# The small constant of an RMS norm as a 129th column of the squares, in a kernel of attention and a gated feed-forward

## What is computed

```python
def _rmsnorm(t, w):
    var = jnp.mean(t * t, axis=-1, keepdims=True)
    return t * jax.lax.rsqrt(var + EPS) * w      # EPS = 1e-06, 128 elements in the last axis
...
q = _rope(_rmsnorm(q, q_norm_w), pos)
k = _rope(_rmsnorm(k, k_norm_w), pos)
```

## Time and profile before

| | us |
|---|---|
| median of 3 runs | 1514.4 |
| lowest and highest | 1512.0, 1514.88 |
| span of the profiled execution | 1372.6 |
| TensorE busy | 1356.7 (99%) |
| VectorE busy | 1204.1 (88%) |
| ScalarE busy | 871.6 (64%) |
| GpSimd busy | 785.0 (57%) |

### The profile page before, as it was taken

The page is one execution under the profiler, slowest core; times in us unless marked ns, Lnnn a source line. Parts: engine busy times, 40 slices in busy tenths (PEclk is TensorE's granted clock), DMA queues, the critical chain, the costliest instruction groups (busy, mean ns, idle before and its releaser), DMA issues.

```text
span 1372.6 us, 23448 instructions
## 1 busy us (share of the span) xinstructions
PE 1356.7 (99%) x8015; PEld 1182.3 (86%) x8015; DVE 1204.1 (88%) x2624; ACT 871.6 (64%) x2224; POOL 785.0 (57%) x813
## 2 busy tenths in 40 slices
PE   8899999999999999999999999999999999999998
PEld 6788888888888888888888888888888888888888
DVE  8999898989898989898989898989899987987783
ACT  7777676767676767676767676767777662222221
POOL 7876766676667666766676667666766510111111
PEclk9999999999999999999999999999999999999999
DMA  6111221111112111211111112112121321111212
GB/s 215 48 53 41 59 55 47 43 59 55 47 43 59 54 47 43 58 55 47 43 59 53 49 42 59 55 47 70 49 72 32 110 96 45 47 47 49 76 40 77
DMA packets 34034, 80.46 MB, mean 59 GB/s; under 512 B 10258, under 2 KB 11538, under 8 KB 32498
## 3 DMA queue, kind: packets, MB, share of 16 engines
q1 hardware_dynamic: 17522, 45.29, 10.5%
q0 software_dynamic: 16384, 33.59, 8.4%
HBM read 76.74 MB, written 2.10 MB: 57 GB/s over the span
## 4 chain that ended last, share of the span: by engine, by line
PE 91%; DVE 5%; ACT 2%; issue 1%; POOL 1%; DMA 0%; DVEq 0%; ACTq 0%
PE proj_ps L111 10%; PE proj_ps L113 10%; PE proj_ps L112 10%; PE turn_ps L770 10%; PE score_ps L113 5%; PE score_ps L112 5%; PE score_ps L111 5%; PE value_ps L111 5%; PE value_ps L112 5%; PE value_ps L113 5%; PE gu_ps L111 3%; PE gu_ps L113 3%; PE gu_ps L112 3%; PE out_ps L1035 2%; PE turn_ps L732 2%; PE turn_ps L739 2%
## 5 line engine op out<-in xcount | busy, mean ns | idle before, releaser
L1286 ACT ACTIVATE probs<-probs,shift,rstd 128x640 f32<-128x640 f32 x256 | 234.4, 917 | 123.3 <-DVE shift L1730 122.2
L561 POOL DMA_INDIRECT kg<-kc,idx x256 | 260.1, 1016 | 83.9 <-issue 78.0
L571 POOL DMA_INDIRECT vg<-vc,idx x256 | 260.0, 1016 | 70.7 <-issue 70.7
L1766 DVE TENSOR_TENSOR pt_lo<-turn_ps,pt_hi 128x512 fp32r<-128x512 f32 x320 | 217.4, 685 | 45.2 <-ACT pt_hi L1292 44.8
L1292 ACT ACTIVATE pt_hi<-turn_ps 128x512 fp32r<-128x512 f32 x320 | 187.5, 593 | 90.6 <-PE turn_ps L770 89.3
L1741 DVE CUSTOM_DVE_ANT_0 probs<-score_ps,mask 128x640 f32<-128x640 f32 x256 | 206.8, 822 | 11.9 <-PE score_ps L113 10.1
L579 POOL TENSOR_TENSOR v_lo<-vg,v_hi 128x512 fp32r<-128x512 f32 x64 | 89.1, 1392 | 207.7 <-ACT v_hi L1257 207.7
L770 PE MATMUL turn_ps<-cst,probs 128*128 128x128 f32 x1280 | 191.5, 272 | 0.7 <-DVE qt_lo L1718 0.7
L111 PE MATMUL proj_ps<-w_hi,xt_parts 128*128 128x512 f32 x496 | 188.9, 381 | 0.0
L770 PEld LDWEIGHTS turn_ps<-cst,probs 128*128 128x128 f32 x1280 | 157.2, 141 | 26.9 <-DVE probs L1759 1.0
L113 PE MATMUL proj_ps<-w_hi,xt_parts 128*128 128x512 f32 x496 | 168.1, 339 | 0.0
(11 more groups left out here) (255 smaller groups left out, 3283.4 us busy)
## 6 DMA issues: line engine op xcount, KB each, us to landing
w_raw<-wqkv SPq DMA_DIRECT2D x28, 384.0 KB, 3.2
wo_raw<-wo SPq DMA_DIRECT2D x32, 256.0 KB, 3.0
wa_sb<-wa SPq DMA_DIRECT2D x7, 1024.0 KB, 4.9
kg<-kc,idx POOLq DMA_INDIRECT x256, 2.6
vg<-vc,idx POOLq DMA_INDIRECT x256
wg_raw<-wg SPq DMA_DIRECT2D x2, 1376.0 KB, 6.1
wu_raw<-wu SPq DMA_DIRECT2D x1, 2752.0 KB, 9.6
wd_raw<-wd SPq DMA_DIRECT2D x1, 2560.0 KB, 12.8
```

Source lines behind the costliest of these rows:

```text
L561: pool.indirect_dma_start(kg[:, b % 2, c, :], None, kc, bass.IndirectOffsetOnAxis(ap=idx[:, s // B % 2, b * NC + c:b * NC + c + 1], axis=0))\
L571: pool.indirect_dma_start(vg[:, b % 2, c, :], None, vc, bass.IndirectOffsetOnAxis(ap=idx[:, s // B % 2, b * NC + c:b * NC + c + 1], axis=0))\
L1286: act.activation(row, row, ACT.Exp, bias=shift[:, h:h + 1], scale=rstd[:, b % 2, h:h + 1], accum_out=sums[:, h:h + 1])\
L1766: dve.tensor_tensor(pt_lo[:, at, :], turn_ps[1 - j % 2][:, :], pt_hi[:, at, :].bitcast(F32), ALU.subtract).then_inc(p_lo_done[j], 1)
```

## The change

Each of the five rows of `qk` gets a 129th element, filled once by GpSimd in the setup with the square root of 128 * EPS. ScalarE squares and sums 129 elements, so the sum in `ss` already holds 128 * EPS. GpSimd's addition, the tensor `ss_eps` and the semaphore `eps_added` go, and the power reads `ss`. The squares of step s now wait for `rstd_done` of the step before in place of `eps_added`, and those of step 0 also for the setup's fills, whose count goes from 4 to 5. The copy of the queries writes four rows of 128 with a gap of one element between them; `squared`, the unused output of the squares, has rows of 129 too. Tensors that lie behind `qk` and `squared` in memory move by 32 or 64 bytes. `eps` stays, since it feeds the dummy activations that load ScalarE's tables.

```diff
--- before.py
+++ after.py
@@ -75,7 +75,7 @@
-SETUP_POOL = 4
+SETUP_POOL = 5
@@ -162,7 +162,6 @@
         squares_done = semaphore("squares_done")
-        eps_added = semaphore("eps_added")
         rstd_done = semaphore("rstd_done")
@@ -230,14 +229,15 @@
             rot_q = sb("rot_q", [P, 2, REP, D])
-            qk = sb("qk", [P, REP + 1, D])
+            qk_eps = sb("qk_eps", [P, REP + 1, D + 1])
+            qk, root_eps = qk_eps[:, :, 0:D], qk_eps[:, :, D:D + 1]
...
-            squared = sb("squared", [P, REP + 1, D], BF16)
+            squared = sb("squared", [P, REP + 1, D + 1], BF16)
@@ -251,7 +251,6 @@
             ss = sb("ss", [P, REP + 1])
-            ss_eps = sb("ss_eps", [P, REP + 1])
@@ -531,6 +530,7 @@
                     pool.memset(eps[:, :], D * EPS).then_inc(setup_pool, 1)
+                    pool.memset(root_eps, math.sqrt(D * EPS)).then_inc(setup_pool, 1)
@@ -584,10 +584,8 @@
                     def norms(s, b):
 
                         wait(pool, squares_done, s + 1)
-                        pool.tensor_tensor(ss_eps[:, :], ss[:, :], eps[:, :], ALU.add).then_inc(eps_added, 1)
-                        wait(pool, eps_added, s + 1)
                         wait(pool, exp_done[REP - 1], s - 1)
-                        pool.tensor_tensor(rstd[:, b % 2, :], ss_eps[:, :], power[:, :], ALU.pow)\
+                        pool.tensor_tensor(rstd[:, b % 2, :], ss[:, :], power[:, :], ALU.pow)\
                             .then_inc(rstd_done, 1)
@@ -1239,7 +1237,7 @@
                         wait(act, squares_done, s)
-                        act.activation(qk[:, 0:REP, :].rearrange("p h d -> p (h d)"), proj_ps[:, :], ACT.Copy)\
+                        act.activation(qk[:, 0:REP, :], proj_ps[:, :].rearrange("p (h d) -> p h d", h=REP), ACT.Copy)\
                             .then_inc(q_copied, 1)
@@ -1257,11 +1255,13 @@
                     def squares(s):
-                        wait(act, eps_added, s)
+                        wait(act, rstd_done, s)
+                        if s == 0:
+                            act.wait_ge(setup_pool, SETUP_POOL)
                         wait(act, q_copied, s + 1)
                         wait(act, kv_copied, s + 1)
                         for h in range(REP + 1):
-                            last = act.activation(squared[:, h, :], qk[:, h, :], ACT.Square, accum_out=ss[:, h:h + 1])
+                            last = act.activation(squared[:, h, :], qk_eps[:, h, :], ACT.Square, accum_out=ss[:, h:h + 1])
                         last.then_inc(squares_done, 1)
```

## The result

The changed kernel takes 1581.5 us (median of 4 runs, 1571.0 to 1589.0) beside 1514.6 us of the kernel before (4 runs, 1512.0 to 1518.1): ratio 1.044, 95% interval 1.040 to 1.048. The forecast was 1513.6 us, and its range ended at 1517.0: it was wrong, and all five rivals were too.

A forecast was written before the change was run, and what follows sets the result against it. TensorE, busy 969 of 970 us in 56 steps, was taken as the bound. Terms: 0 in the steps, -0.8 us in the opening, 0 in the feed-forward part; 1514.4 - 0.8 = 1513.6 us, range 1510.8 to 1517.0.

The forecast's parts named there:

- all five rivals: Opening untangles, 1511.3 (0.10); power blocks VectorE, 1538 (0.05); layout costs, 1519 (0.05); opening tangles, 1515.3 (0.06); no effect, 1514.4 (0.12).
- The span lies 141.8 us under the median of the runs, and nothing of the change is outside it: Whole kernel: the traced span of 1372.6 us plus a constant 141.8 us gives the run time, the change touching only the span.
- Worth 0 us from step 8 on: Ordinary steps: GpSimd saves 0.27 to 0.70 us per step without its addition, which goes into v_lo's wait for v_hi; 0 us.
- The new wait of the squares: ScalarE's squares wait for the power of the step before, with over 13 us of margin; 0 us.
- the 129th column: ScalarE's squares: one element more costs at most 2.3 ns each, hidden in ScalarE's waits; taken as 0.
- the gap between heads: Copy of the queries out of PSUM and VectorE's reads: runs with 4-byte gaps cost nothing; taken as 0.
- The rule of the two sides: SBUF ports of GpSimd and VectorE: whoever starts first holds them throughout; by it the price would be rival 2's, 1538 us at most.
- Rival 2: Each step: the earlier power blocks VectorE's L1689 for 1.04 us, at most 25 us in all, 1538 us; chance 0.05.
- The opening: First steps: three norms 0.27 us earlier each bring table products 0.8 us earlier, cutting TensorE's 1.58 us stall to 0.8; -0.8 us.
- the chain of 0.27 us steps: Opening: norms 0, 1 and 2 give about 0.27 us each, so table products, shifts and pt_lo come 0.8 us earlier.
- I expect the next encounter to repeat: Opening, 53.87 us: v_lo meets rotation L1682 again, which takes 2.12 us, and TensorE's 1.34 us stall at 56.96 stays.
- rival 4: Opening tangles worse: earlier GpSimd instructions meet another VectorE pair, one more stall up to 1.7 us; +0.9 us, 1515.3; chance 0.06.

The follow-up runs named there:

- spent_add: Changed kernel, with GpSimd again spending the addition's time ahead of the power on a result nobody reads: 1490.6 us, ratio 1.002 to the kernel before.
- k_wait: Changed kernel, with the four gathers of cached keys waiting from step 4 on for the signal of j=4's transposes: 1384.1 us, ratio 0.929 to the kernel before.
- before_again: The kernel before, unchanged, run and traced again: ratio 1.000; its profiled execution took 1486.8 us with a span of 1484.9.
- after_again: The changed kernel once more, on one chip with three variants of it: 1540.1 us, ratio 1.032 to the kernel before.
- layout_only: The kernel before with qk in rows of 129, squares still over 128 and the addition kept: ratio 0.999.
- k_wait_all: Changed kernel, with the gathers of cached keys waiting for j=4's signal from step 1 on: 1377.0 us, ratio 0.924 to the kernel before.
- k_wait_all_before: The kernel before, addition kept, with its gathers of cached keys waiting for j=4's signal from step 1 on: 1374.4 us, ratio 0.923.
- after: The changed kernel's trace from the first comparison, span 1587.1 us; the kernel took 1581.5 us there, ratio 1.044 to the kernel before.
- before: As a trace: the kernel before, unchanged, as the prediction read it, span 1372.6 us; the kernel took 1514.6 us in the first comparison.

## Why the prediction was wrong, step by step

**"The span lies 141.8 us under the median of the runs, and nothing of the change is outside it" failed first.** The span of a usual execution lies 1.9 us under its time, so the 141.8 us were not outside the span. They were stalls in the steps, of the kind the change acts on. The traced execution had none of them, and why it had none no run here shows. The missing 9% were the sign that the trace was not of the kernel as it is timed; adding them back as a constant turned an open question into a term of the sum.

**"Worth 0 us from step 8 on" failed with it.** Its local half held: the power fell to 1.20 us, the norm ended 0.7 us earlier, and nobody waited for it. But it followed the saving to GpSimd's own wait at v_lo and went past the eight gathers on the way, which all move with it, as things that only take time. In the usual execution their place decides: 1.2 us ahead of the transposes of j=4 they leave the signal of j=4 late by 1.5 us, 2.0 us ahead they leave that of j=3 late by 1.8 and that of j=4 by 3.4. spent_add shows it by putting GpSimd's time back with all else of the change kept, k_wait by moving only the gathers. From before_again to after_again the longer steps make up the whole loss (63 us by the steps, 61.1 by the spans), with the lower clock behind the longer stops in it. On the chip of the result the loss was 67 us; there is no trace of a usual execution of the kernel before from there, so for that figure the account is argued and not shown.

**The new wait of the squares (0 us), the 129th column (0) and the gap between heads (0)** were right: layout_only is at 0.999, squares take 300 ns, no wait for the power shows, and spent_add has all three and a ratio of 1.002.

**The rule of the two sides.** The prediction set the pair at 90.03 against a sentence of the Trainium skill (SBUF — State Buffer, section "SBUF: two separate sides") by which whoever starts first has the shared ports for its whole instruction; the pair at 620.99 disagrees with it again, 0.68 us for L1689 begun 0.20 us into the power, and so do all 39 such pairs of that trace (0.67 to 0.68 us). Rival 2 fell as argued. The prediction also called v_lo against L1682 an agreement. By its own rows that is not shown: L1682 had begun 0.10 us ahead of v_lo, and it was still the one that took 2.12 us.

**The opening (-0.8 us) failed in sign.** Where the transposes' signals are on time, k_wait_all against k_wait_all_before puts the change at +2.6 us. The 1.58 us at 43.63 of the earlier trace rows did not shrink to 0.8 when the norms came earlier: k_wait_all has 1.61 there, in front of the product with the values and no longer of the turn of the keys. k_wait_all_before, however, has 0.37 at that place where before_again, with the same code until step 1, has 1.90, so this stretch moves by more than the term from one trace to the next, and the chain of 0.27 us steps drawn through it was not one that could be followed. The step "I expect the next encounter to repeat" failed too: with the norms earlier it was L1681 that met GpSimd's table products, for 3.52 us, and the stop behind it was 2.72 us in k_wait_all (2.24 in after) and not 1.34. That is rival 4's mechanism, which had a chance of 0.06. The +2.6 us can't be laid to this stop alone, since the first transposes of j=4 stand 2.2 us apart already (41.99 and 44.19), and before_again has them at 44.89.

**The rivals** shared the forecast's mistake. They asked which engine is next in line for time or for the memory port, and none asked what else runs while these gathers are issued. That is why no chance was left above 1538 us.

What stays open is why a gather holds up signals of TensorE, and why at these places. In the trace of the changed kernel the gathers of values beside the transposes of j=1 and j=2 leave those signals on time, and k_wait's gathers leave j=3 and j=4 on time but not the scores behind them.

One rival stands untested: that the recording of an execution has a part in it. Each timed run here comes with a recorded span and clock, so no run shows how the kernel does without recording. The traces also differ in how complete they are. That of before holds 14853 semaphore records, 8173 of the 8192 landings of gathers among them; all the others hold 7923 to 9469, with over half of the landings missing in the fullest of them (3766 in k_wait_all_before). The missing records are no mark of the stalls, for k_wait_all has 9361 and no late transposes. But the one complete trace is also the only one in which gathers stood beside these transposes (1.2 us ahead) and every signal came on time.

## What to carry to other kernels

Compare the span of the profiled execution with the time of the runs before anything else: if they differ by more than a few us, the trace is of another execution, and its stalls are not those that are timed. An instruction that looks free can hold others in a good place, so when something goes from an in-order engine, list what moves with it and what runs beside it there, above all gathers issued by GpSimd. If a signal comes late beside such gathers, tie their start to an event behind it: one wait here took 1488.6 us to 1374.4, where GpSimd had 7.6 us of idle time in each step of 19.06 us to pay for it (before_again, 110 to 1080 us).

## What the runs showed of the hardware

- A signal of TensorE can reach the waiting engine 3.8 us late in the changed kernel, while matmuls go on being put out, and the signals held back can come together, within 0.11 us. It goes with indirect gathers that GpSimd issues at that moment: four that start 2.0 us ahead to 1.9 us behind the transposes of j=4 give 1.8 and 3.4 us on the mean at j=3 and j=4, one at 2.0 us ahead gives 0.5 at j=3, four from 0.4 or from 1.5 us behind on give none at either, and instead 0.53 us at j=0 or 0.75 us at the first scores.
- It does not go by the rows a gather moves: 32 rows and 128 rows of 512 bytes do the same (1.047 and 1.032 to 1.044), and GpSimd issues them in 935 and 985 ns on the mean.
- The same program took 1514.6 us in the one comparison and 1486.6 to 1492.0 in the others, and one traced execution of it has a span of 1372.6, which is within 0.2 us of that of k_wait_all_before, 1372.4: the time without late transposes.
- After TensorE's stop of 2.21 us the granted clock was 0.51 for some 3 us (615 to 618 us). In before_again, where such a stop is 1.17 us in the step at 561 us, its mean over the steps is 1.00.
- VectorE's rotation L1681 (128x512) took 3.52 us in k_wait_all in place of 0.68, against GpSimd's table products, while L1689 (128x512) begun during GpSimd's power of 128x5 kept its 0.68 us.
